# Alternating the query chunks of an attention kernel, with fp32r masks, a deeper probability ring and two transfers of the maxima

## What is computed

```python
q, k = rope(q), rope(k)                          # (1, 32, 1024, 16)
scores = einsum('bhqd,bhkd->bhqk', q, k) / sqrt(16)
scores = where(causal, scores, -inf)
y = einsum('bhqk,bhkd->bhqd', softmax(scores), v)
# layer 0 adds the attention to 10 adapter tokens before its projection
x = layernorm(x + y @ w_proj)
x = layernorm(x + lookup(x))
x = layernorm(x + attention_1(x))
x = layernorm(x + swiglu(x))
```

## Time and profile before

| | us |
|---|---|
| median of 3 runs | 1120.79 (1120.6 to 1121.11) |
| the profiled execution | 1121.8 |
| its span, first to last instruction | 1119.9 |
| first exponential to last result copy, layer 0 | 292.35 |
| the same, layer 1 | 290.40 |
| TensorE busy | 1007.8 |
| VectorE busy | 643.8 |
| ScalarE busy | 486.3 |
| GpSimd busy | 228.5 |

### The profile page before, as it was taken

How to read it: one execution, slowest core, us unless ns; L and a number is a source line. 1 busy time by engine, 2 the same in 40 slices (tenths; PEclk the granted TensorE clock), 3 DMA queues, 4 the chain that set the end, 5 groups by cost and what they waited for, 6 DMA issues and landing times. The chain is left out here.

```text
span 1119.9 us, 15914 instructions
## 1 busy us (share of the span) xinstructions
PE 1007.8 (90%) x5974; PEld 620.4 (55%) x5974; DVE 643.8 (57%) x1151; ACT 486.3 (43%) x750; POOL 228.5 (20%) x457
## 2 busy tenths in 40 slices
PE   7787998999999999798777799999999988889998
PEld 4455874555544543484354555555445435767766
DVE  6441543455778884384844444567888833835464
ACT  4220323342267676522632133422666774346740
POOL 3222002222111212106132022211111123012300
PEclk9995975555589998997879655555899999989999
DMA  9553081222221200200015511211112001051101
GB/s 306 168 176 118 1 181 41 60 74 53 70 53 48 69 22 2 94 1 1 0 55 182 171 23 45 52 42 48 31 30 59 3 2 38 1 176 57 38 20 57
DMA packets 39774, 74.75 MB, mean 67 GB/s; under 512 B 6512, under 2 KB 8368, under 8 KB 39696
## 3 DMA queue, kind: packets, MB, share of 16 engines
q1 hardware_dynamic: 39696, 73.70, 22.5%
HBM read 50.29 MB, written 22.87 MB: 65 GB/s over the span
## 5 line engine op out<-in xcount | busy, mean ns | idle before, releaser
L973 DVE TENSOR_REDUCE mx<-psum 128x1 f32<-128x512 f32 (+3 forms) x640 | 373.0, 631 | 163.0 <-PE psum L857 139.4
L926 ACT ACTIVATE arena_p<-psum 128x1024 f32<-128x1024 f32 (+3 forms) x384 | 292.8, 809 | 301.6 <-PE psum L872 299.8
L849 PE MATMUL psum<-k_st,q_st 48*128 48x512 f32 (+3 forms) x768 | 312.1, 505 | 10.6 <-PEq L242 4.0
L849 PEld LDWEIGHTS psum<-k_st,q_st 48*128 48x128 f32 x768 | 168.9, 246 | 141.4 <-DVE mx L973 120.9
L872 PE MATMUL psum<-q_st,k_st 50*128 50x512 f32 (+3 forms) x768 | 227.0, 479 | 8.7 <-ACT arena_p L926 5.6
L891 PE MATMUL psum<-arena_p,v_grp 128*32 128x512 f32 (+3 forms) x1536 | 203.3, 609 | 9.9 <-POOL arena_p L1013 8.8
L1013 POOL TENSOR_SCALAR_AFFINE_SELECT arena_p<-arena_p 128x256 f32<-128x256 f32 x256 | 101.2, 409 | 295.9 <-ACT arena_p L926 290.5
L872 PEld LDWEIGHTS psum<-q_st,k_st 50*128 50x128 f32 x768 | 127.9, 233 | 48.2 <-ACT arena_p L926 37.2
L855 PE MATMUL psum<-maskb,pick 64*128 64x128 bf16 x512 | 132.8, 289 | 0.0
L857 PE MATMUL psum<-maskb,pick_high 64*128 64x64 bf16 x512 | 109.1, 231 | 0.0
L257 PE MATMUL psum<-x_h,w 128*128 128x512 f32 x224 | 89.2, 462 | 10.6 <-DVE w L482 7.4
(11 more groups left out here) (200 smaller groups left out, 1153.8 us busy)
## 6 DMA issues: line engine op xcount, KB each, us to landing
q_parts<-arena_p SPq DMA_DIRECT2D x48, 256.0 KB
q_st<-q_parts SPq DMA_DIRECT2D x64, 192.0 KB, 4.0
k_parts<-arena_p SPq DMA_DIRECT2D x30, 256.0 KB
k_st<-k_parts SPq DMA_DIRECT2D x32, 200.0 KB
k_st<-k_parts SPq DMA_DIRECT2D x16, 400.0 KB
ff_raw<-in_w_in SPq DMA_DIRECT2D x11, 512.0 KB, 3.5
arena_w<-in_w SPq DMA_DIRECT2D x12, 256.0 KB, 5.7
ff_wd_raw<-in_w_down SPq DMA_DIRECT2D x1, 2560.0 KB, 11.8
```

The source lines that it names most:

```text
L849: last = pe.matmul(psum[:, bank, width * n:end], q_st[rows, s, p, P * i:P * i + P], k_st[rows, s, key_pair(p), 512 * kc:512 * kc + width], ...
L926: act.activation(pr[:, n % NP_RING, :, o:512], psum[:, 2 * (n % 2):2 * (n % 2) + 2, o:512], ACT.Exp, scale=scale).then_inc(exp_ready, 1)
L973: dve.tensor_reduce(mx[:, b % 2, kc, col:col + 4 * len(heads) - 3:4], src, AX, ALU.max)\
```

## The change

The pieces of the diff, in the order of the text to come:

- `steps` runs over g outside and c inside, so that units alternate between c=0 and c=1; the loads (`load`) follow, and the places where the join is made and waited for.
- `pick`, `pick_high` and `maskb` become fp32r; `maskb` gets a buffer of its own.
- TensorE's order now goes by two key tiles: scores of the tile two ahead (p=0, p=1), scores p=0 of the one three ahead, values of one tile, values of the next, scores p=1. Due entries of the maxima's list are still issued between them, also between the two value products.
- NP_RING = 8: four more probability buffers, in the place of xT.
- Entry T is the fourth of its list instead of the third; the result copy stands after the fourth exponential of the next unit instead of the second.
- The maxima are laid out so that two DMAs per unit carry them instead of four.

```diff
-NP_RING = 4
+NP_RING = 8
-        pick = at("pick", M_ID + 512, [P, P], BF16)
-        pick_high = at("pick_high", M_SMALL + 9472, [P, P], BF16)
-        maskb = at("maskb", M_ID + 768, [P, P], BF16)
+        pick = at("pick", M_ID + 512, [P, P], F32R)
+        pick_high = at("pick_high", M_SMALL + 9472, [P, P], F32R)
+        maskb = stack.enter_context(nc.sbuf_tensor("maskb", [P, P], F32R))
...
-        c, g = divmod(u, NG)
+        g, c = divmod(u, CH)
...
-    pr = view(arena_p, 0, [NP_RING, 2, 512])
+    pr = [view(a, 4096 * n, [2, 512]) for a in (arena_p, arena_x) for n in range(NP_RING // 2)]
...
-    steps = [(c, g) for c in range(CH) for g in range(NG)]
+    steps = [(c, g) for g in range(NG) for c in range(CH)]
...
-            out.insert(min(2, len(out)), "T")
+            out.insert(min(3, len(out)), "T")
...
+    blocks = [(u, kt) for u, (c, _) in enumerate(steps) for kt in range(n_tiles[c])]
...
                 for t in range(2):
-                    for j in range(2):
-                        row = 64 * t + KS + j
-                        sp.dma_start(q_st[row:row + 1, s, :, :].bitcast(F32)
-                                     .rearrange("o p n -> o (p n)").rearrange("o (i q) -> o i q", q=P),
-                                     mT[16 * j + 8 * t:16 * j + 8 * t + 8, u % 2, :])\
-                            .then_inc(max_loaded[s], 16)
+                    sp.dma_start(q_st[64 * t + KS:64 * t + KM, s, :, :].bitcast(F32)
+                                 .rearrange("j p n -> j (p n)").rearrange("j (i q) -> j i q", q=P),
+                                 mT[16 * t:16 * t + 16, u % 2, :]).then_inc(max_loaded[s], 16)
...
-            scores(0, 0, 0)
-            scores(0, 0, 1)
-            for u in range(NU):
-                c = steps[u][0]
+            for u, kt in blocks[0:2]:
+                for p in range(2):
+                    scores(u, kt, p)
+            for u, (c, _) in enumerate(steps):
                 todo = lists[u + 2] if u + 2 <= NU else []
                 n_slots = 4 * n_tiles[c]
                 issued = 0
-                for slot in range(n_slots):
-                    kt, part = divmod(slot, 4)
-                    ahead = (u, kt + 1) if kt + 1 < n_tiles[c] else (u + 1, 0)
-                    if part < 2 and ahead[0] < NU:
-                        scores(*ahead, part)
-                    if part == 3:
-                        values(u, kt)
-                    while issued < (len(todo) if u + 2 == NU else len(todo) * (slot + 1) // n_slots):
+
+                def maxima(slot):
+                    nonlocal issued
+                    while issued < (len(todo) if u + 2 == NU else len(todo) * slot // n_slots):
                         entry(first_entry[u + 2] + issued, u + 2, todo[issued])
                         issued += 1
+
+                at = blocks.index((u, 0))
+                for n in range(0, n_tiles[c], 2):
+                    ahead = blocks[at + n + 2:at + n + 4]
+                    for k, (au, akt) in enumerate(ahead):
+                        for p in range(2 - k):
+                            scores(au, akt, p)
+                            maxima(4 * n + 2 * k + p + 1)
+                    values(u, n)
+                    maxima(4 * n + 5)
+                    values(u, n + 1)
+                    maxima(4 * n + 7)
+                    if ahead:
+                        scores(*ahead[1], 1)
+                    maxima(4 * n + 8)
...
-                    if u and b == 1:
+                    if u and b == 3:
                         copy_o(u - 1)
...
-                    if n == 1 and b > NG:
+                    if n == 1 and b and steps[b - 1][0] == 1:
                         join_max(b - 1)
```

43 lines of the change are left out of this document (23 added, 20 removed).

## The result

The changed kernel takes 1294.57 us (median of 4 runs, 1286.33 to 1299.28) against 1120.69 for the kernel before on the same chip: a ratio of 1.156, 95% interval 1.148 to 1.163. The forecast was 1094 us in a range of 1056 to 1150, so it is wrong in sign and by 200 us.

The account below looks back on a forecast made before the run. TensorE was taken to bound c=0 units at half clock, TensorE and VectorE together c=1 units. Start, seven c=0 and c=1 pairs and last units gave -16.0 and -11.1 us per layer, together -27.1: 1094 us, range 1056 to 1150.

Parts of the forecast that it names:

- the price of a c=1 unit: Attention units with c=1: reached by neither new wait, a third of the cold-start difference added, 20.5 us, ends 19.3 and 22.1.
- the slower rival: The clock is lost in every c=0 unit: 39.1 us per c=0 and c=1 pair, 1151 us by the median; chance 0.30.
- c=0 units, 14.5 us: Attention units with c=0: new waits and some units losing the clock in part, 14.5 us, ends 12.5 and 17.0.
- The chain: In a c=0 unit, mask wait, value product, transpose, maxima transfer, next scores and seven reductions follow one another: 13.5 to 14 us.
- Masks at nothing: fp32r mask matmuls on TensorE: loads can run under the matmul before, so no gain or loss; range widened 10 us each way.
- the 123 us bound: Upper bound on the fp32r masks' cost: 1024 mask matmuls at 0.12 us more per weight load, if each were bare.
- Two-tile runs and eight buffers at nothing: TensorE's value products: not adjacent, so no tile-shape change saved except in the last two units; eight buffers also taken as nothing.
- The later copy at nothing: The result copy moved two exponentials later: 0.59 us on ScalarE, busy 13.42 of 19.73 us, so nothing.
- Start, end, two transfers: Starts +8 and +11 us; last c=0 unit 10, last c=1 unit 13.33; transfers issued in 1.3, issue and landing 2.2.
- The fast one: Rival that the clock holds throughout: 32.3 us per c=0 and c=1 pair, 1056 us by the median; chance 0.20.
- a busy share of 58%: TensorE in the new c=0 unit: busy about 8 us of 13.9, so some units lose the clock in part.
- The forecast's own case: Some c=0 units lose the clock in part: pair of c=0 and c=1 34 to 36.5 us, 1075 to 1115; chance 0.42.

Follow-up runs that it names:

- e12: The kernel before with four useless 128-column matmuls ahead of the first value product of each c=0 unit; 1083.53 us, ratio 0.965.
- e11: e2 with GpSimd making the first two masks of a c=0 unit before the split of the next maxima and the copy of values; 1097.69 us.
- e2: The kernel before with the units alternating and nothing else; 1228.3 us, against 1132.14 for the kernel before on the same chip.
- e14: The changed kernel with its scores spread as in e7, plus eight useless matmuls in each c=0 unit; 1242.89 us.
- e8: e2 with eight useless 128-column matmuls before the first value product of each c=0 unit; 1043.92 us, ratio 0.928 to the kernel before.
- e1: The kernel before with the fp32r masks alone; 1151.15 us, ratio 1.021.
- e17: e8 with fp32r masks; 1057.74 us.
- e3: The changed kernel with bf16 masks put back; 1251.73 us, ratio 1.109 to the kernel before.
- e18: e14 with bf16 masks; 1188.45 us.
- e7: e5 with the score steps spread between the value products, still two key tiles ahead; 1141.14 us, ratio 1.012 to the kernel before.
- e4: The changed kernel with the old order of units, all c=0 then all c=1; 1273.39 us, ratio 1.131 to the kernel before.
- e5: The changed kernel with the old order of units and bf16 masks; 1259.39 us, ratio 1.118 to the kernel before.
- e6: e5 with TensorE's old order as well; 1277.92 us, ratio 1.138 to the kernel before.
- e9: e6 with the result copy back after the second exponential; 1139.72 us, ratio 1.015 to the kernel before.

## Why the prediction was wrong

**What bounds the kernel.** Right that the clock is the largest lever, wrong in what I then did with it. I read that c=0 units run at half clock and asked what they would do in the new order. e12 shows the other reading: half clock is no property of these units; with four matmuls at their one wait of 0.87 us they take 10.5 us. The row was there, and I used it as a small cost at half clock and did not ask what the clock had to do with it. Whether the wait or the amount of work decides is open: e11, without the wait, has units at either clock.

**The step that failed: the price of a c=1 unit.** I took 20.5 us with an upper end of 22.1, because the one unit that starts cold in the trace of before takes 22.11 us. That row shows a recovery after 5.8 us of half clock; it says nothing of a unit in which the recovery fails or comes late, and I took it for certain that each c=1 unit brings the clock back. The runs show units wholly at half clock at 31.8 us (e2), 32.8 with fp32r masks (e14), 34.6 in the changed kernel. The bound could have been had from the same rows: clock 0.87 over 22.11 us is 5.75 us at half clock, and they cost 22.11 - 19.73 = 2.38 us, 0.41 us each; a unit wholly at half clock then takes 19.73 / 0.59, some 33.5 us. In the changed kernel the 14 c=1 units that I had at 20.5 took 206.0 and 211.4 us a layer instead of 143.5: 130 of the 205 us that the two attentions, without their starts, stand above my sum. The Trainium skill, "TensorE: Matmul & The Clock Gate", section "A second HAM failure mode: psum-queue depth-cycling", describes short idles between groups of matmuls that make the clock swing ("HAM" is its name for the block that sets the clock). This case looks the same, with waits of 0.6 to 1.6 us and units of 26.5 to 34.6. For the slower rival I had cited Part 1 of that page of the Trainium skill, that activity releases the clock. The traces bear this out in part: added work brought the clock back in e8 and e12, but units in which TensorE is recorded as busy throughout stay at half clock (31.80 of 31.80 us, e2). I had priced that rival at 39.1 us per pair; measured pairs are 45 to 52, and 56 the first of layer 1.

**c=0 units, 14.5 us.** Measured 18.0 to 19.1, and 21.9 the first: 63 us over my sum in both layers. The chain was right where it can be read at full clock: in e14 the first value product begins 4.7 us after the last one of the unit before (I had 4.3 from a point close by), the maxima lie in SBUF at 7.8 (6.9), the next scores start at 10.4 (9.1 to 9.5), all from the same point. Wrong was the loss of clock in part: 16.7 to 19.1 us of each at half clock, and the end of 17.0 was too low: it lies under the old 15.33 plus the 2.5 us of waits that I named (17.8), and holds nothing for masks and score waits.

**Masks at nothing.** The cost lies on the upper side, which I had left open, but beyond what I allowed for. Weight loads of the changed kernel, beside the 124 ns of L855:

```profile
L858 PEld LDWEIGHTS psum<-maskb,pick_high 64*128 64x128 f32 x512 | 126.2, 286 | 6.5
L856 PEld LDWEIGHTS psum<-maskb,pick 64*128 64x128 f32 x512 | 124.0, 288 | 1.1
```

(The mean depends on the clock: at nearly the clock of the kernel before it is 275 ns in e1.) The direct cost is 0.6 us per unit (e1; 0.2 in the c=0 units of e17): 17 us in e1 and 14 between e8 and e17, about a seventh of the 123 us bound; the rest of the load's time doesn't show in the units. My 10 us each way did not even hold this. What I left out is the indirect cost: with the longer loads the clock returns later or less often (e3: 43 us, e14 against e18: 54 us).

**Two-tile runs and eight buffers at nothing.** That the two products are not adjacent and save nothing was right (e7's unit is 0.2 us shorter). I looked at the products and not at the scores: three score steps against two pairs of banks. This was countable in the diff without any price: the order's third step needs an exponential that has only just begun. It costs 2.8 us per c=1 unit at full clock (e4 against e1), and the clock (e5 against e7, 118 us).

**The later copy at nothing.** ScalarE's time was the wrong thing to look at; the copy frees bank 6 for TensorE. With scores two tiles ahead the trace shows no wait for it (e7), without them it costs 138 us (e6 against e9).

**Start, end, two transfers.** Starts +5 and about +9 against +8 and +11. The last c=0 unit 10.8 and 11.7 against 10; the last c=1 unit 18.8 and 17.7 against 13.33, which I took over unchanged: 13.7 and 9.1 us of these two are at half clock, and their scores are bunched too (e7: 11.4 with spread scores). The two transfers are issued in 1.28 us, as taken; from issue to use they take 2.6 us in e14 (I had 2.2).

**The rivals.** The slower one named the mechanism, the clock lost in the c=0 units, but let the c=1 units recover it. The range was also drawn too low for it: I wrote that it leaves out a third of this case, yet the case's own sum, 1151 us, lies above the range's end of 1150. The fast one, "the clock holds", is a real state of the same order of units: e8 reaches 30.4 us per pair. Which of the two comes true was decided by 1.7 us of work at one place per c=0 unit (an estimate of the run's forecast), where I had weighed a busy share of 58%. The forecast's own case, one third of a loss, is not what any of the runs settles on.

## What to carry to other kernels

Where a trace shows stretches at half clock, ask first whether they have to be there, and test it with a few useless matmuls in the short waits of TensorE before changing anything else: here four of them were worth 3.5% and eight, with the alternating order, 7.2%. Price each edit that adds a wait to TensorE not by its length but by the unit's time at the other clock, in full, until a run shows that the clock returns. And count, for a new order of an in-order queue, the buffers that each step needs at its place (PSUM banks, result bank), not only those the edit enlarges.

## What the runs showed of the chip that I had not expected

- A TensorE without a recorded gap can stay at 1.2 GHz: 31.80 us busy of 31.80 at clock 0.50 (e2, the row above), and e9 has four units in a row of 32.1 to 32.3 us; the same unit at full clock is busy 18.77 of 19.08 us (e8). A c=0 unit at full clock with TensorE busy 10.15 of 10.51 us keeps it (e12), one at half clock with 14.46 of 15.33 doesn't get it back. e11's c=0 unit does both, 9.06 of 9.09 us at full clock and 14.45 of 14.45 at half. In these rows the busy share at half clock says nothing on whether the clock will return. One possible reason, not tested, is that the ends of matmuls are modelled.
- The clock makes one program two: four runs of e2 lie between 1200.61 and 1261.12 us, of e11 between 1040.94 and 1174.46.
- An fp32r mask weight load of 128 columns, 64 rows deep, takes 275 ns against 124 for bf16 (e1 and the kernel before, mean over both clocks; 207 against 100 where nearly all of the run is at full clock, e17 and e8); 32 such loads make a c=0 unit 0.6 us longer at half clock and 0.2 at full, and a c=1 unit 0.6 us longer at full clock.
